# Attention times values in the switch-head layers: plain fp32 with the turned probabilities as the stationary operand

## The reference

```
gate_v, gate_o = top-2 of 8 experts per head, normalised sigmoids      # [s, 8 heads, 8 experts]
q, k = x @ q_w[h].T, x @ k_w[h].T                                      # 128 wide per head
v    = sum_e gate_v[s,h,e] * (x @ v_w[h,e])
att  = softmax(q k^T / sqrt(128))                                      # 384 x 384 per head
ctx  = att @ v                                                         # 384 x 128 per head
out  = sum_h,e (ctx[s,h] * gate_o[s,h,e]) @ o_w[h,e]
```

## Time and profile before

| | us |
|---|---|
| median of 3 runs | 831.9 (831.78 to 832.63) |
| the profiled execution, its own time | 830.64 |
| its span, first to last instruction | 828.3 |
| PE busy | 812.1 (98%) |
| DVE, ACT, POOL busy | 488.8, 375.4, 463.7 |

### The profile page before, as it was taken

One profiled execution on the slowest core, in us unless ns is written; L12 is line 12 of the kernel. 1 busy time (PEld: TensorE's weight loads), 2 busy tenths in 40 slices (PEclk: granted clock), 3 DMA queues, 4 the chain that ended last, 5 costly groups with the idle time before them and its releaser, 6 DMA issues.

```text
span 828.3 us, 13610 instructions
## 1 busy us (share of the span) xinstructions
PE 812.1 (98%) x4743; PEld 658.8 (80%) x4743; DVE 488.8 (59%) x1108; ACT 375.4 (45%) x614; POOL 463.7 (56%) x297
## 2 busy tenths in 40 slices
PE   4999999999999999999999999999999999999998
PEld 4999998889998789898678678578578578588476
DVE  6998873444443247898644554654655645645544
ACT  5333336556655352334624634524634534534531
POOL 4577765433334436557564665564665665665652
PEclk9999999999999999999999999999999999999999
DMA  8666663533222339533498498497597597697684
GB/s 281 196 181 196 194 191 107 171 106 101 76 76 76 102 109 323 179 116 132 126 229 326 111 256 289 117 258 280 126 268 261 130 263 262 138 255 262 145 217 173
DMA packets 66176, 153.36 MB, mean 185 GB/s; under 512 B 9392, under 2 KB 22320, under 8 KB 66128
## 3 DMA queue, kind: packets, MB, share of 16 engines
q1 hardware_dynamic: 51472, 120.73, 42.0%
q0 software_dynamic: 10944, 24.82, 16.4%
q10 hardware_dynamic: 3712, 7.18, 3.4%
HBM read 122.06 MB, written 37.97 MB: 193 GB/s over the span
## 4 chain that ended last, share of the span: by engine, by line
PE 82%; DMA 5%; issue 4%; POOL 4%; DVE 3%; ACT 1%; POOLq 0%; SPq 0%; DVEq 0%; ACTq 0%
PE bank L1513 21%; PE bank L1515 20%; PE bank L1514 20%; PE bank L1799 12%; PE bank L1560 5%; POOL mask_scratch L471 4%; DMA mask_scratch<-scratch,cell 4%; PE bank L1623 2%; PE bank L1597 2%; DMA x<-in_x 1%; DVE scratch L950 1%; DMA mask<-mask_scratch 0%; ACT scratch L616 0%; DVE hT_lo L895 0%; ACT scratch L681 0%
## 5 line engine op out<-in xcount | busy, mean ns | idle before, releaser
L522 POOL TENSOR_TENSOR w_lo<-w_raw,w_hi 128x1024 fp32r<-128x1024 f32 x69 | 171.2, 2482 | 139.4 <-ACT w_hi L763 137.5
L1513 PE MATMUL bank<-w_hi,hT_hi 128*128 128x512 f32 (+1 forms) x504 | 196.0, 389 | 0.1
L1515 PE MATMUL bank<-w_hi,hT_lo 128*128 128x512 f32 (+1 forms) x504 | 194.1, 385 | 0.0
L1514 PE MATMUL bank<-w_lo,hT_hi 128*128 128x512 f32 (+1 forms) x504 | 193.7, 384 | 0.0
L467 POOL TENSOR_TENSOR w_lo<-w_raw,w_hi 128x1024 fp32r<-128x1024 f32 x39 | 95.1, 2440 | 103.6 <-ACT w_hi L604 82.6
L763 ACT ACTIVATE w_hi<-w_raw 128x1024 fp32r<-128x1024 f32 x86 | 90.9, 1057 | 134.8 <-PE bank L1515 104.2
L1515 PEld LDWEIGHTS bank<-w_hi,hT_lo 128*128 128x128 f32 x504 | 94.7, 188 | 19.1
L1513 PEld LDWEIGHTS bank<-w_hi,hT_hi 128*128 128x128 f32 x504 | 94.8, 188 | 18.6 <-issue 0.6
L1513 PE MATMUL bank<-hT_hi,w_hi 128*128 128x384 f32 x320 | 107.8, 337 | 1.7 <-DVE hT_lo L895 1.7
L1514 PEld LDWEIGHTS bank<-w_lo,hT_hi 128*128 128x128 f32 x504 | 94.8, 188 | 17.5
L1515 PE MATMUL bank<-hT_hi,w_lo 128*128 128x384 f32 x320 | 107.0, 334 | 0.0
(11 more groups left out here) (209 smaller groups left out, 1289.6 us busy)
## 6 DMA issues: line engine op xcount, KB each, us to landing
w_raw<-in_units SPq DMA_DIRECT2D x145, 512.0 KB, 4.0
late<-in_units SPq DMA_DIRECT2D x56, 512.0 KB, 7.9
scratch<-slots_scratch SPq DMA_DIRECT2D x7, 512.0 KB, 6.8
scratch<-in_src_row ACTq DMA_DIRECT2D x8, 384.0 KB, 4.2
scratch<-in_dst_row ACTq DMA_DIRECT2D x8, 384.0 KB, 5.5
sums_scratch<-zeros SPq DMA_DIRECT2D x1, 1536.0 KB, 8.2
sums_scratch<-x SPq DMA_DIRECT2D x1, 1536.0 KB, 9.2
x<-sums_scratch SPq DMA_DIRECT2D x3, 512.0 KB, 4.5
```

Of the source, the lines that this page charges most:

```text
L522: pool.tensor_tensor(w_lo[:, s, :], w_raw[:, s, :], w_hi[:, s, :].bitcast(fp32), ALU.subtract).then_inc(lo_ready[s], 1)
L1513: pe.matmul(dst, a_hi, b_hi, start=first, stop=False)
L1514: pe.matmul(dst, a_hi, b_lo, start=False, stop=False)
L1515: return pe.matmul(dst, a_lo, b_hi, start=False, stop=last)
```

## The change

- `f_norm_of`, `fv_hi_of`, `fv_lo_of`, `f_pT_lo_of`, `context_of` and `context_turns` go. The turned exponentials are copied by ACT as plain fp32 (`f_pT`).
- `f_attend` becomes nine plain-fp32 matmuls with a 128x128 block of `f_pT` stationary and 128 columns of the summed values moving. The context comes out token-major, in bank 0 (`CONTEXT`).
- The division by the row sums moves to the gates: `f_scale_of` makes `row_scale` (heads 0 to 6) or `last_gates` (head 7), and `gate_rows_of` and `gate_context` use them.
- The waits follow: the turns of the probabilities wait for the exponentials, `f_attend` for the gated values and `f_pT`, the gates for `f_attend` itself.

```
-                pe.wait_ge(fv_lo_done, head + 1)
-                for m in range(NT):
-                    pe.wait_ge(f_pT_lo, head * NT + m + 1)
-                    last = three(bank[context_bank(head)][:, 0:N], v2_hi[:, m, :],
-                                 v2_lo[:, m, :], pT_hi[:, m, :], pT_lo[:, m, :], m == 0, m == NT - 1)
+                pe.wait_ge(v_gated, head * 6 + 6)
+                pe.wait_ge(f_pT_done, head * NT + NT)
+                for t in range(NT):
+                    tok = slice(t * P, (t + 1) * P)
+                    for m in range(NT):
+                        last = pe.matmul(bank[CONTEXT][:, tok], f_pT[:, m, tok], v_sum[:, m, :], start=m == 0,
+                                         stop=m == NT - 1)
                 last.then_inc(f_context, 1)
-            def context_turns(h):
-                pe.wait_ge(context_ready, h + 1)
-                for t in range(NT):
-                    last = turn(bank[turned_bank(h)][:, t * P:(t + 1) * P], context[:, t * P:(t + 1) * P])
-                last.then_inc(context_T, 1)
...
                 f_attend(h)
-                output_round(h - 1, 4)
-                context_turns(h)
-                for r in range(5, SLOTS):
+                for r in range(4, SLOTS):
                     output_round(h - 1, r)
...
-            def f_norm_of(head):
+            def f_scale_of(head):
                 dve.wait_ge(f_exp, head * NT + NT)
                 step.add(dve.reciprocal(inv_sum[:, 0:NT], row_sum[:, 0:NT]))
                 settled()
-                for t in range(NT):
-                    dve.tensor_scalar(F[:, t, :], F[:, t, :], inv_sum[:, t:t + 1], None,
-                                      ALU.mult).then_inc(f_norm, 1)
+                if head < FH - 1:
+                    for k in range(2):
+                        scale_of = best[:, 4 + k, :].rearrange("p (t g) -> p t g", t=NT)
+                        step.add(dve.tensor_tensor(row_scale[:, k, :], inv_sum[:, 0:NT], scale_of[:, :, FH + head],
+                                                   ALU.mult))
+                else:
+                    step.add(dve.tensor_tensor(last_gates[:], gates[:, :, (GROUPS - 1) * FE:GROUPS * FE],
+                                               inv_sum[:, 0:NT].unsqueeze(2).to_broadcast([P, NT, FE]), ALU.mult))
...
             def gate_rows_of(h):
-                dve.wait_ge(context_T, h + 1)
+                dve.wait_ge(f_context, h + 1)
...
-                        dve.tensor_scalar(gated_rows[:, k, t, :], bank[turned_bank(h)][:, t * P:(t + 1) * P],
-                                          scale_of[:, t, FH + h:FH + h + 1], None, ALU.mult).then_inc(gated_rows_ready, 1)
+                        dve.tensor_scalar(gated_rows[:, k, t, :], bank[CONTEXT][:, t * P:(t + 1) * P],
+                                          row_scale[:, k, t:t + 1], None, ALU.mult).then_inc(gated_rows_ready, 1)
```

More of the change, by code:

```diff
@@ L99, in k_bank @@
     return 1 if h == 1 else 7
[L102 to L107, removed]
+CONTEXT = 0
 def act_rows(n):
@@ L185, in gnn_switch_kernel @@
         k2_hi, k2_lo = sb("k2_hi", [P, N], f32r), sb("k2_lo", [P, N], f32r)
-        v2_hi, v2_lo = sb("v2_hi", [P, NT, P], f32r), sb("v2_lo", [P, NT, P], f32r)
-        pT_hi, pT_lo = sb("pT_hi", [P, NT, N], f32r), sb("pT_lo", [P, NT, N], f32r)
+        f_pT = sb("f_pT", [P, NT, N], fp32)
+        row_scale = sb("row_scale", [P, 2, NT], fp32)
+        last_gates = sb("last_gates", [P, NT, FE], fp32)
         gcT = sb("gcT", [P, 2, HALF], fp32)
@@ L743, in f_exp_of, with f_pT_of @@
                                    scale=FFN_SCALE, accum_out=row_sum[:, t:t + 1]).then_inc(f_exp, 1)
[L745 to L749, removed]
+            def f_pT_of(head):
+                if head:
+                    act.wait_ge(f_context, head)
                 for m in range(NT):
                     act.wait_ge(f_probs_T, head * NT + m + 1)
[L752 to L756, removed]
+                    act.activation(f_pT[:, m, :], bank[TF[m]][:, 0:N], ACT.Copy).then_inc(f_pT_done, 1)
             def hi_ring(*name):
@@ L820, in _ @@
             hi_ring("v", 1, 0)
-            f_pT_hi_of(0)
-            fv_hi_of(0)
+            f_pT_of(0)
             for h in range(1, FH):
@@ L835, in _ @@
                 hi_ring("v", h, 6)
-                f_pT_hi_of(h)
+                f_pT_of(h)
                 copy_out(h - 1, 1)
@@ L1278, in gate_values @@
                 dve.wait_ge(unit_used, need)
+                if head and g == 0:
+                    dve.wait_ge(f_context, head)
                 for ts in ((0,), (1, 2)):
@@ L1414, in _ @@
             f_max_of(0)
-            f_norm_of(0)
+            f_scale_of(0)
             copy_ranks()
@@ L1437, in _ @@
                     find_experts()
-                f_norm_of(h)
                 gate_values(h, 0, R["v", h, 3] + 1)
-                f_pT_lo_of(h)
+                f_scale_of(h)
                 make_hots(h - 1)
@@ L1452, in _ @@
                 copy_out(h - 1, 10)
-                fv_lo_of(h)
                 y_out(h - 1, 3)
@@ L1466, in gate_context @@
                 if e == 0:
-                    dve.wait_ge(context_T, FH)
+                    dve.wait_ge(f_context, FH)
+                    settled()
                     dve.wait_ge(gated_rows_landed, 16 * 6 * (FH - 1))
@@ L1470, in gate_context @@
                     dve.wait_ge(gated_T, e - 1)
-                c = (GROUPS - 1) * FE + e
                 dve.tensor_tensor(gated[:, e % 2, :].rearrange("p (t d) -> p t d", t=NT),
-                                  bank[turned_bank(FH - 1)][:, 0:N].rearrange("p (t d) -> p t d", t=NT),
-                                  gates[:, :, c:c + 1].to_broadcast([P, NT, P]), ALU.mult).then_inc(gated_ready, 1)
+                                  bank[CONTEXT][:, 0:N].rearrange("p (t d) -> p t d", t=NT),
+                                  last_gates[:, :, e:e + 1].to_broadcast([P, NT, P]), ALU.mult).then_inc(gated_ready, 1)
             def gc_lo_of(e):
@@ L1714, in f_scores_of, with f_probs_of @@
                           True).then_inc(f_scores, 1)
-            def f_probs_of(head, banks=TF):
-                pe.wait_ge(f_norm, head * NT + NT)
+            def f_probs_of(head):
+                pe.wait_ge(f_exp, head * NT + NT)
                 for m in range(NT):
                     for t in range(NT):
-                        last = turn(bank[banks[m]][:, t * P:(t + 1) * P], F[:, t, m * P:(m + 1) * P])
+                        last = turn(bank[TF[m]][:, t * P:(t + 1) * P], F[:, t, m * P:(m + 1) * P])
                     last.then_inc(f_probs_T, 1)
             def f_attend(head):
-                pe.wait_ge(fv_lo_done, head + 1)
-                for m in range(NT):
-                    pe.wait_ge(f_pT_lo, head * NT + m + 1)
-                    last = three(bank[context_bank(head)][:, 0:N], v2_hi[:, m, :],
-                                 v2_lo[:, m, :], pT_hi[:, m, :], pT_lo[:, m, :], m == 0, m == NT - 1)
-                last.then_inc(f_context, 1)
-            def context_turns(h):
-                pe.wait_ge(context_ready, h + 1)
-                for t in range(NT):
-                    last = turn(bank[turned_bank(h)][:, t * P:(t + 1) * P], context[:, t * P:(t + 1) * P])
-                last.then_inc(context_T, 1)
+                pe.wait_ge(v_gated, head * 6 + 6)
[5 more added lines that the diff above has]
+                                         stop=m == NT - 1)
+                last.then_inc(f_context, 1)
             def rank_outputs():
@@ L1846, in _ @@
                     value_unit(h, 6)
-                pe.wait_ge(f_pT_lo, NT * (h + 1))
+                pe.wait_ge(f_pT_done, NT * (h + 1))
                 pe.wait_ge(slots_landed, 16 * h)
```

27 lines of the change are left out of this document (4 added, 23 removed).

## The result

The changed kernel takes 833.92 us (median of 8 runs, 832.32 to 835.35), the kernel before 831.84 beside it: ratio 1.0026, 95% interval 1.0017 to 1.0035. The forecast, 833.4, is 0.5 under the first median and 0.2 under the second.

A forecast was written before the change was run, and what follows sets the result against it. PE's own sequence was taken to bound the kernel. Heads 1 to 6 +1.56, head 7 -0.22 and head 0 +0.16 gave +1.5 on 831.9, so 833.4 us; own range 832.6 to 834.2, full range 830.2 to 835.4.

The forecast's parts named there:

- The view that decided: Round 7, heads 1 to 6: waits for DVE's copy of round 5; PE gains 0.14 us, waits the other 0.48.
- The attention: PE, heads 1 to 7: 18 plain-fp32 records at 0.110 us take 2.18 in place of 1.78, 0.40 more.
- Rival 2: Attention: loads of 128 plain-fp32 columns are not hidden, distance near 0.21 us; 15 us more, 848.5; chance 0.08.
- rival 4: Attention: records start every 0.08 us, faster than the passes allow; 4.3 us less, 829.1; chance 0.04.
- The turns: Between rounds 4 and 5, heads 1 to 7: removing the context's turns frees 0.62 us of PE.
- Heads 1 to 6: Attention's +0.40 less 0.14 recovered before round 7: +0.26 us a head, +1.56 for six heads.
- Heads 0 and 7: Head 0: +0.16 us net; head 7, where DVE's chain is not the limit: -0.22.
- At nothing: Work taken from DVE and ACT, small multiplications added on DVE and PE's new waits change no time.
- sign (f): In the profile after, DVE is some 3 us less busy per head, with no effect.
- rival 1: Heads 1 to 6: the wait doesn't bite and round 7 starts on its slot; -1.4 us, 830.5; chance 0.15.
- rival 3: DVE's chain to the copy of round 5 gets 0.2 to 0.5 us longer; 834.6 to 836.4; chance 0.10.
- rival 5: PE's own pace rises as DVE and ACT read PSUM less; -1.6 us, 831.8 with the forecast; chance 0.07.

The follow-up runs named there:

- e1: Changed kernel with DVE's copy of round 5 put ahead of the six gates in heads 1 to 6: 829.81 us, ratio 0.9991 to the kernel before.
- e3: Changed kernel with three unused turns of the unit matrix on PE between rounds 4 and 5, heads 0 to 6: 835.08 us, ratio 1.0046.
- e2: Kernel before the change, with DVE's copy of round 5 put ahead of the six gates: 831.71 us, ratio 1.0003.
- e6: Changed kernel with the nine plain-fp32 attention matmuls of each head done twice: 849.81 us, one run.
- e5: Changed kernel with six unused 128x384 multiplications added on DVE in each head: 834.19 us, ratio 1.0028 to the kernel before.
- e7: Changed kernel, attention of heads 1 to 6 behind round 7, gates behind copies of rounds 5 to 7, ACT's round 3 copy earlier: 828.46 us, ratio 0.9960.
- e8: The changed kernel unaltered, run again among the follow-up runs: 833.56 us, ratio 1.0024 to the kernel before.
- e4: Changed kernel, attention of heads 1 to 6 behind round 7, gates behind copies of rounds 5 to 7, ACT's order kept: 831.50 us, ratio 1.0002.

## Why the prediction was right, step by step

- **The view that decided.** PE's rows of before show no wait in the rounds. The sequencer's 2050 ns, laid on the loads and on DVE's copy, gave a slack of 0.14. Measured: from the start of round 4 to that of round 7 5.79 became 5.63, so 0.16 was recovered, and 0.46 (0.87 between two records where 0.41 is usual) was lost; forecast 0.14 and 0.48. e1 and e3 show both from the other side: taking the copy from behind the gates gives back 0.48, putting 0.62 of work on PE costs only 0.10; e2 shows that the kernel before had no such wait to give back. This step is shown.
- **The attention.** 18 records at 0.112, first load exposed (0.214 to the second record), 0.205 on leaving: 2.20, forecast 2.18. With 1.79 before, the attention costs 0.42 more, forecast 0.40. The pace of 0.110 came from the router's fp32r row and from the columns of the graph layer; both held. Rival 2 (0.21 a record) and rival 4 (0.08 a record) fall: e6 gives 0.112 over 18 further records. About 81 ns is what the Trainium skill ("TensorE: Matmul & The Clock Gate", section Back-to-back issue gap) gives at 128 columns; this trace does not agree with it, neither for plain fp32 (0.112) nor for fp32r (0.11), and the measurement decides.
- **The turns.** Round 5 starts 1.74 behind round 4 in place of 2.33, and in e1, where nothing waits, round 7 starts 5.17 behind round 4 in place of 5.79: 0.62 freed, as forecast.
- **Heads 1 to 6: mis-sized.** Forecast +0.26 a head, 1.56 in all; measured +0.30 to +0.32 in five of them, 2.00 in all. The attention brings 0.42 in place of 0.40, the recovered slack -0.16, the first slot of round 7 behind the wait is 0.02 longer, together 0.28. The other 0.01 to 0.04 of a head is spread over a few starts in the dense units that come 0.01 later each; why is not shown. In head 2 the wait before round 7 was 0.155 longer once (PE restarts 0.35 behind DVE's copy in place of 0.20, while DVE is on time); the second trace has it in head 1, that of e5 in none. What it is stays open. So the term "net for each of heads 1 to 6" was too small by 0.05 on average, and six times that with the one late restart is the 0.44 by which this term fell short.
- **Heads 0 and 7.** +0.14 and -0.14 for +0.16 and -0.22. In head 7 the attention cost 0.42 and the turns gave back 0.62, as forecast; the missing 0.06 is not placed. Head 7 had no gap, since there are no six gates in its chain, as the earlier trace rows said.
- **At nothing.** DVE's relief was larger than sign (f) said (37.7 us, 4.7 a head, for some 3) and worth nothing in heads 1 to 7 (e5); head 0 is the place where it is not free to give it back. That ACT's relief was worth nothing is argued from its idle time and not tested. None of the change's own new waits stands in PE's list of waits.
- **Rivals 1, 3 and 5.** The wait bit (rival 1 would be a period of 61.09, which is what e1 shows with 61.13). DVE's chain kept its 2.76 (rival 3). PE's pace in the rest of a head did not rise (rival 5): from the end of the rounds to the next rounds it takes 45.43 before and 45.44 to 45.47 after.
- **The chances.** The forecast lay 0.2 under the border to "slower", and 0.36 of its 0.56 were put on "no change". With 2.0 in place of 1.56 - 0.22 + 0.16 = 1.5 the ratio comes out just on the other side (0.26% and 0.24%, with intervals that reach down to 0.17% and 0.16%). The mechanism was right, and on which side of that border the time fell hung on 0.5 us. That the second median is only 0.2 from the forecast is luck: the two medians of that set are 1.65 apart, while its ratio and the traces say 2.0.

## What to carry to other kernels

When work is taken from the bounding engine, what it then meets early is the result of another engine; read from the sequencer's wait and the releaser's end how much slack there was, since no row of the busy engine shows it, and move what stands ahead of that result (here one copy before six multiplications turned +2.0 us into -1.1, by the traces). After each such move look for the next engine whose pause the moved work had been: putting the attention behind the rounds gained less than that one move (457.9 against 457.2) until ACT's copies stood in the order in which PE needs them (455.4). Keep work of one array shape together: the two changes around the attention, from the four-lane form to the full array and back, cost 0.3 us a head together (e1 against e7).

## What the runs showed of the hardware that was not expected

- **The start of a run comes in two kinds, 2 us apart.** In the first dense unit fp32r matmuls over 384 columns start every 0.17 us in some profiles and every 0.32 in others, whatever the kernel: at 0.17 from the start in before, e3 and e8, at 0.32 for 8 to 12 matmuls in after, e1, e2, e4, e5, e6 and e7 (in e7 only after six at 0.17). The changed kernel, its first profile and that of e8:

```profile
17.10 0.69 PE L1488 MATMUL bank<-hT_hi,w_hi 128*128 128x384 f32 x1 [1.47 <-DVE hT_lo L875]
17.58 0.52 PE L1489 MATMUL bank<-hT_lo,w_hi 128*128 128x384 f32 x1
17.90 0.52 PE L1490 MATMUL bank<-hT_hi,w_lo 128*128 128x384 f32 x1
```

```profile
17.03 0.45 PE L1488 MATMUL bank<-hT_hi,w_hi 128*128 128x384 f32 x1 [1.60 <-DVE hT_lo L875]
17.31 0.34 PE L1489 MATMUL bank<-hT_lo,w_hi 128*128 128x384 f32 x1
17.49 0.33 PE L1490 MATMUL bank<-hT_hi,w_lo 128*128 128x384 f32 x1
```

  In both PE had idled some 1.5 us and had done short turns before. 384 columns in 0.32 us are 1.2 a nanosecond, the pace of the lower of the two levels (1.2 GHz). The granted clock shows it only in part: for the window 15 to 21.5 us it reads 0.74 to 0.75 in e4, e6 and e7, but 1.00 in after, e1, e2 and e5. So it is likely the lower level of the clock, met at another moment from run to run; what decides it is not shown. It is why parts of two traces are compared from behind it. In the run times a similar split can be seen: of 21 runs of the kernel before on one chip, 7 lie between 830.4 and 831.0 and 14 between 831.7 and 833.0. That the start makes this split is shown only as far as traces go: the profiled executions of before, e3 and e8, with the fast start, are at or near the fastest of their sets.
- **Plain fp32 with 128x128 blocks runs at 0.112 us a record, two records a matmul**, the pace of one fp32r matmul over 128 columns: the 128-column load adds nothing that can be seen to the distance (e6). One product of a 128x128 block with 128 columns costs 0.22 so; by the same pace three fp32r parts over 128 columns would cost 3 x 0.112 = 0.34 (an estimate from the earlier trace rows). But the kernel before moved 384 columns at a time, 0.173 a matmul, and so paid 3 x 0.173 for three such products, 0.17 each. That is why nine plain-fp32 matmuls took longer than nine fp32r ones.
